# Stage one of a fused four-layer kernel written in another order: values four batches behind, block splits in two parts, later tables, two more banks

## The chip, the core and the metric

The kernel runs on one core of one Trainium2 chip. The time is that of the device in microseconds (us); lower is better. The profile comes from one profiled execution of the program, and its times count from the start of the span.

## The reference

Input x has 8 batches of 128 tokens with 512 features. Four layers are added to it one after the other. All arithmetic is fp32; the kernel builds each fp32 product from rounded parts (below).

```python
x = x + _L0_cond_ref(x, L0_cond_weight, itok_B_3_7)     # einsum('bsi,boi->bso', x, weight[ids]): one 512x512 weight for each batch
x = x + _L1_cond_ref(x, mask, pos, itok_B_0_7, wq, wk, wv, wo, aq, bq, ak, bk, av, bv, ao, bo)
x = x + _L2_cond_ref(x, A, B, itok_B_3_7)               # a rank-16 pair for each batch
x = x + _L3_cond_ref(x, itok_B_0_23, W, b, lora_As, lora_Bs)
...
def _L1_cond_ref(...):                                   # attention, 32 query heads, 8 key/value heads, D = 128
    q = lora_linear(x, wq, aq, bq, ids)                  # x @ w + (x @ a[ids]) @ b[ids]
    k = lora_linear(x, wk, ak, bk, ids)
    v = lora_linear(x, wv, av, bv, ids)
    q, k = apply_rope(q), apply_rope(k)                  # needs cos and sin of the positions
    ...                                                  # masked softmax(q k^T) v, then lora_linear(o, wo, ao, bo, ids)
```

## The kernel before, in words

The program has four parts, each an instruction block that all engines leave together. Stage one (up to about 118 us) computes layer L0 for the 8 batches and turns the result into what attention reads, and it also computes half of v. Stage two projects the rest of v and all of k. Then comes a loop over the 8 key/value heads, and last the layers L2 and L3. The change touches only stage one.

An fp32 product is built from three matmuls in the type fp32r: high x high, high x low, low x high. The high part of a tile is a copy by ScalarE (ACT), the low part is the difference, by VectorE (DVE) or GpSimd (POOL). In stage one the work on batch `b` is:

- SyncE (SP) loads x of the batch (`x_row(b)`, the tensor `res`), the batch's own 1 MB weight (`w0_raw`, shown as `w_raw`) and its adapter (`a_raw`). The weight has two buffers, so the load of batch b waits until the splits of batch b-2 are done.
- TensorE (PE) turns x (`turn_x`, into `ps_x`), ACT and DVE split it (`split_x`). ACT splits the four quarters of the weight; DVE takes the low part of quarters 0 and 2, POOL of 1 and 3 (`split_w`, both write `wt_lo`).
- `product`: 12 matmuls into `ps_y`. `add` (DVE, writes `res`): x1 = x + product. `turn_x1` (PE) and `split_x1` (ACT, DVE) give x1 turned, in two parts.
- `adapters` (PE, 12 matmuls of 48 columns, into `ps_a`), `pack_ax` (DVE, `axn`), `turn_ax` (PE), `copy_axt` (ACT, `axt_q`, `axt_k`, `axt_v`).
- `values`: PE runs `v_tile`, 13 matmuls of 512 columns into `ps_v`, ACT takes `v_hi`, DVE takes `v_lo`, SP stores both (`store_v`).

`v_tile` of batch 0 to 7 multiplies with block 0 of wv. A block is 1 MB of weight (`raw_w`, split into `blk_hi` and `blk_lo`) and 1 MB of adapter packs (`raw_b`, eight loads, split into `blk_b`: ACT one copy and DVE one `low_copies` on L169 for each of four packs). `block_part(0)` is this split of block 0, `block_part(1)` that of block 1, which stage two reads first. In block 1 the same tensors appear as `wt_x` and `wt_lo`. The rotation tables are computed by `angles` (DVE, four parts), two Sin activations (ACT), and the mask by `mask_table` (DVE).

The order is written out by hand: on each engine a loop over `b` calls these functions, and an engine does its instructions in that order. So whatever stands ahead of an instruction on its engine holds it up, however early its own inputs are. In the kernel before, PE does in iteration b: `turn_x(b + 1)`, `product(b)`, `turn_ax(b - 2)`, `adapters(b - 1)`, `values(b - 2)`, `turn_x1(b)`.

## Time and profile before

| | |
|---|---|
| time, median of 3 runs | 799.65 us (797.23 to 800.19) |
| the profiled execution: time | 800.8 us |
| the profiled execution: span | 799.1 us |
| PE busy in the span | 736.8 us (92%) |
| mean granted PE clock | 0.97 of full speed |
| stage one ends, first matmul of stage two | 118.20 us |

The page gives busy time by engine. For a change in one stage its rows are read by stage: what each engine did between two times, what it waited for, and in what order of time. A wait of PE in the middle of a stage costs its length only if PE is what the stage waits for later as well.

### The profile page before, as it was taken

The page shows a single profiled execution, that of the slowest core. Times are in us where ns is not written, and L with a number is a line of the kernel's source. Part 1 is how long each engine was busy: PE and PEld are TensorE (multiplying, and loading weights), DVE is VectorE, ACT ScalarE, POOL GpSimd, SP SyncE. Part 2 cuts the span into 40 slices and gives each one's busy share as a digit, 9 for nine tenths or more (in the row PEclk, how much of TensorE's full clock was granted, in tenths as well). Part 3 has the DMA queues.
Part 4 walks back from the last instruction along what each step waited for, and adds up shares of the span by engine and source line. Part 5 has one row for each costly group of instructions (what it writes and reads, how often), then busy time and mean ns, then how long its engine had stood idle before and what let it go on. Part 6 is the DMA issues. An engine that isn't in the chain of part 4 may idle for free. (4 is left out here: it accounts for less than half of the span.)

```text
span 799.1 us, 14134 instructions
## 1 busy us (share of the span) xinstructions
PE 736.8 (92%) x4392; PEld 646.8 (81%) x4392; DVE 549.0 (69%) x1468; ACT 328.0 (41%) x980; POOL 288.4 (36%) x242
## 2 busy tenths in 40 slices
PE   3597979998789999999999999999999999986898
PEld 2476858787679989998999998989999999876686
DVE  4667544688587676767677668767676767754973
ACT  3525343211154363445345445345445434443540
POOL 3322213245273254245236235325434522410510
PEclk9879979999899999999999999999999999999899
DMA  8557157865214024122212403402402112500402
GB/s 287 196 182 230 53 157 204 244 226 191 71 53 126 1 74 134 47 73 101 76 45 80 125 0 125 125 0 81 143 25 72 52 46 57 123 13 28 109 27 79
DMA packets 61435, 81.56 MB, mean 102 GB/s; under 512 B 21158, under 2 KB 38694, under 8 KB 57814
## 3 DMA queue, kind: packets, MB, share of 16 engines
q1 hardware_dynamic: 60482, 79.80, 32.2%
q0 software_dynamic: 768, 1.25, 0.6%
q8 instruction: 18, 0.29, 0.2%
q14 instruction: 19, 0.16, 0.1%
q10 hardware_dynamic: 148, 0.07, 0.0%
HBM read 66.13 MB, written 15.48 MB: 102 GB/s over the span
## 5 line engine op out<-in xcount | busy, mean ns | idle before, releaser
L1000 POOL TENSOR_TENSOR prob<-prob,rinv 128x512 f32<-128x512 f32 x64 | 66.7, 1042 | 199.7 <-DVE rinv L1090 199.7
L949 ACT ACTIVATE prob<-sm,nmax 128x128 f32<-128x128 f32 x256 | 99.8, 391 | 70.1 <-DVE nmax L1071 70.1
L1175 PE MATMUL ps_out<-wt_x,v_hi 128*128 128x272 f32 x512 | 112.8, 301 | 5.1 <-DVE v_lo L1043 2.7
L993 POOL TENSOR_TENSOR qt<-qc,qs 128x512 f32<-128x512 f32 x60 | 77.6, 1293 | 107.2 <-DVE qs L1026 107.2
L1179 PE MATMUL ps_out<-wt_x,v_lo 128*128 128x272 f32 x512 | 106.4, 289 | 0.0
L1177 PE MATMUL ps_out<-wt_lo,v_hi 128*128 128x240 f32 (+1 forms) x512 | 103.2, 283 | 0.0
L77 PE MATMUL ps_q<-x1t_hi,blk_hi 128*128 128x512 f32 x240 | 100.6, 419 | 0.0
L935 ACT ACTIVATE v_hi<-ps_o 128x512 fp32r<-128x512 f32 x64 | 38.1, 596 | 149.8 <-PE ps_o L1155 149.8
L79 PE MATMUL ps_q<-x1t_hi,blk_lo 128*128 128x512 f32 x240 | 95.7, 399 | 0.0
L78 PE MATMUL ps_q<-x1t_lo,blk_hi 128*128 128x512 f32 x240 | 95.6, 398 | 0.0
L1175 PEld LDWEIGHTS ps_out<-wt_x,v_hi 128*128 128x128 f32 x512 | 79.9, 190 | 9.3 <-DVE v_lo L1043 4.3
L1026 DVE TENSOR_TENSOR qs<-ps_q,sin_t 64x512 f32<-64x512 f32 x120 | 82.7, 689 | 3.7
L1177 PEld LDWEIGHTS ps_out<-wt_lo,v_hi 128*128 128x128 f32 x512 | 81.1, 190 | 0.0
L1179 PEld LDWEIGHTS ps_out<-wt_x,v_lo 128*128 128x128 f32 x512 | 79.6, 190 | 0.0
L1071 DVE CUSTOM_DVE_ANT_0 sm<-ps_s,maskbias 128x128 f32<-128x128 f32 x256 | 59.0, 286 | 29.6 <-issue 29.0
L1137 PEld LDWEIGHTS ps_s<-kt,qt 128*128 128x128 f32 x512 | 67.2, 193 | 11.4 <-issue 6.5
L1137 PE MATMUL ps_s<-kt,qt 128*128 128x128 f32 x512 | 68.4, 277 | 5.2 <-PEq L655 5.2
L929 ACT ACTIVATE v_hi<-ps_t 128x512 fp32r<-128x512 f32 x64 | 38.2, 597 | 43.6 <-PE ps_t L1145 43.6
L1050 DVE TENSOR_TENSOR res<-ps_out,res 128x272 f32<-128x272 f32 x128 | 49.9, 431 | 8.9 <-PE ps_out L1179 8.9
L79 PEld LDWEIGHTS ps_q<-x1t_hi,blk_lo 128*128 128x128 f32 x240 | 45.5, 190 | 10.9
L1039 DVE TENSOR_TENSOR v_lo<-ps_t,v_hi 128x512 fp32r<-128x512 f32 x64 | 44.1, 689 | 14.0 <-ACT v_hi L929 13.5
L77 PEld LDWEIGHTS ps_q<-x1t_hi,blk_hi 128*128 128x128 f32 x240 | 45.9, 191 | 8.3
(217 smaller groups left out, 1571.1 us busy)
## 6 DMA issues: line engine op xcount, KB each, us to landing
wo_raw<-in_L_cond_wo_l SPq DMA_DIRECT2D x8, 1024.0 KB, 4.7
raw_w<-in_L_cond_wq_l SPq DMA_DIRECT2D x8, 1024.0 KB, 5.3
raw_b<-in_L_cond_bq SPq DMA_DIRECT2D x64, 128.0 KB, 2.9
w_raw<-in_L_cond_weight_t SPq DMA_DIRECT2D x7, 1024.0 KB, 6.1
v_hi_d<-v_hi SPq DMA_DIRECT2D x16, 256.0 KB, 2.7
v_lo_d<-v_lo SPq DMA_DIRECT2D x16, 256.0 KB, 3.3
k_rot<-kr SPq DMA_DIRECT2D x16, 256.0 KB, 2.9
kt<-k_rot SPq DMA_DIRECT2D x16, 256.0 KB, 2.7
```

The source lines that it names most:

```text
L77: pe.matmul(bank[:, :], w_hi[:, k, cols], x1t_hi[:, k, tok], start=(k == 0), stop=False)
L78: pe.matmul(bank[:, :], w_hi[:, k, cols], x1t_lo[:, k, tok], start=False, stop=False)
L79: pe.matmul(bank[:, :], w_lo[:, k, cols], x1t_hi[:, k, tok], start=False, stop=False)
L949: e = act.activation(prob[i][:, h, :], sm[:, h, :], ACT.Exp, bias=nmax[i][:, h:h + 1], scale=-1.0, accum_out=rsum[i][:, h:h + 1])
L993: pool.tensor_tensor(qt[:, half, h, :], qc[:, :], qs[:, :], ALU.add).then_inc(q_done, 1)
L1000: pool.tensor_tensor(prob[i][:, :, :], prob[i][:, :, :], rinv[i][:, :].unsqueeze(2).broadcast_to([P, G, T]), ALU.mult).then_inc(prob_done, 1)
L1026: dve.tensor_tensor(qs[to:to + 64, :], ps_q[i][at:at + 64, :], sin_t[to:to + 64, tok], ALU.mult).then_inc(q_mult, 1)
L1071: m = dve.tensor_tensor_reduce(out=sm[:, h, :], in0=ps_s[i][:, h, :], in1=maskbias[:, b, :], scale=-1.0, scalar=3.0e38, op0=ALU.add, op1=A ...
L1137: mm = pe.matmul(ps_s[b % 2][:, h, :], qt[:, half, h, at:at + T], kt[:, b * T:(b + 1) * T], start=True, stop=True)
L1175: pe.matmul(ps_out[i][:, :], ot_hi[:, q], wo_x[:, h, wide], start=(h == 0), stop=False)
L1177: pe.matmul(bank, ot_hi[:, q], wo_lo[:, h, cols], start=False, stop=False)
L1179: mm = pe.matmul(ps_out[i][:, :], ot_lo[:, q], wo_x[:, h, wide], start=False, stop=(h == G - 1))
```

## The change

No computation is added or left out. Stage one is written in another order:

- `values` runs four batches behind (`LAG = 4`) where it ran two behind. The last four batches' tiles go to the two banks of `ps_y` in place of `ps_v`, since the products are over by then.
- `block_part` is cut into `block_w_part` (the weight) and `block_b_part` (the packs). For block 0 they stand in iterations 2 and 3 (both stood in 1), for block 1 in iterations 8 and 9 (both in 8), and behind the values of the iteration on ACT and DVE.
- SP loads x of batch 1 ahead of the weight of batch 1; the adapters and x of 2 and 3 next; block 0's weight behind the weight of batch 2; block 0's packs behind that of batch 3; block 1 behind that of batch 6.
- `angles` has one part in each of iterations 4 to 7 (two in each of 2 and 3); the two Sin activations stand in iteration 9 (4); `mask_table` in 10 (5).

```diff
+        LAG = 4
...
+            v_bank = [ps_v] * LAG + [ps_y[n % 2] for n in range(LAG, B)]
...
+                        if b == 0:
+                            sp.dma_start(x_row(1), x[1]).then_inc(x_in[1], 16)
                         if b == 1:
-                            for n in (1, 2, 3):
-                                sp.dma_start(x_row(n), x[n]).then_inc(x_in[n], 16)
-                            load_block_w(sp, 0)
                             sp.wait_ge(ids_in, 32)
                             picks.extend(...)
                             load_a(0)
                             load_a(1)
-                            load_block_b(sp, 0, picks)
+                            for n in (2, 3):
+                                sp.dma_start(x_row(n), x[n]).then_inc(x_in[n], 16)
                         if b == 2:
+                            load_block_w(sp, 0)
                             for n in range(4, B):
                                 sp.dma_start(x_row(n), x[n]).then_inc(x_in[n], 16)
                         if b >= 2:
                             load_a(b)
-                        if b == 5:
+                        if b == 3:
+                            load_block_b(sp, 0, picks)
+                        if b == 6:
                             sp.wait_ge(raw_lo_done, KC // 2 + PAIRS)
                             sp.wait_ge(raw_lo_pool, KC // 2)
                             load_block_w(sp, 1)
                             load_block_b(sp, 1, picks)
-                        if b >= 4:
-                            sp.wait_ge(v_lo_done, b - 3)
-                            store_v(sp, b - 4)
-                    for n in range(B - 4, B):
+                        if b >= LAG + 2:
+                            sp.wait_ge(v_lo_done, b - LAG - 1)
+                            store_v(sp, b - LAG - 2)
+                    for n in range(B - LAG - 2, B):
...
-                        if b == 1:                                  # POOL: block_lo(1, 0), block_lo(3, 0)
+                        if b == 3:
...
-                        else:                                       # PE, values(b)
+                        elif b < LAG:
                             pe.wait_ge(v_lo_done, b)
+                        elif b >= LAG + 2:
+                            pe.wait_ge(v_lo_done, b - 1)
                         pe.wait_ge(axt_done, 3 * b + 3)
-                        v_tile(pe, ps_v, 0, b, v_ready)
+                        v_tile(pe, v_bank[b], 0, b, v_ready)
...
-                        if b >= 2:
-                            values(b - 2)
+                        if b >= LAG:
+                            values(b - LAG)
...
                         if b == B:                                  # ACT
-                            block_part(1)
-                        if b >= 2:
-                            values(b - 2)
+                            block_w_part(1)
+                        if b == B + 1:
+                            block_b_part(1)
...
-                        if b == 1:
-                            block_part(0)
-                        if b == 4:
+                        if b == 2:
+                            block_w_part(0)
+                        if b == 3:
+                            block_b_part(0)
+                        if b == B + 1:
                             act.wait_ge(tab, 8)                     # then the two Sin activations
...
-                        if b in (2, 3):                             # DVE
-                            angles(2 * (b - 2))
-                            angles(2 * (b - 2) + 1)
-                        if b == 5:
+                        if 4 <= b < 8:
+                            angles(b - 4)
+                        if b == B + 2:
                             mask_table()
```

The queue of SP at the start of stage one, from the weight of batch 1 on, before (`res` is x, `raw_w` block 0's weight; L273 are loads of the adapter ids into registers, of which two of eight stand here):

```order
L267 DMA w_raw<-in_L_cond_weight_t 128x2048
L270 DMA res<-in_x 128x512 x3
L150 DMA raw_w<-in_L_cond_wv_l 128x2048
L273 TENSOR_LOAD id_rows
L273 ISA x2
L273 TENSOR_LOAD id_rows
```

The same queue in the changed kernel, from the second adapter load (`a_raw`) on:

```order
L256 DMA a_raw<-in_L_cond_a_qkv 128x192
L280 DMA res<-in_x 128x512 x2
L262 TENSOR_LOAD id_rows
L262 ISA x2
L271 DMA w_raw<-in_L_cond_weight_t 128x2048
L150 DMA raw_w<-in_L_cond_wv_l 128x2048
L284 DMA res<-in_x 128x512 x4
```

Block 0's weight now stands behind the weight of batch 2; before, it and all eight pack loads stood ahead of it.

DVE before, from the end of iteration 1 (`x1t_lo` of batch 1) to the sum x1 of batch 2 (`res`) and the tables:

```order
L509 TENSOR_TENSOR x1t_lo<-ps_x1turned,x1t_hi 128x4x128
L514 TENSOR_TENSOR a_lo<-a_raw,a_hi 128x192
L565 TENSOR_TENSOR blk_lo<-raw_w,blk_hi 128x512 x2
L169 SCALAR_TENSOR_TENSOR blk_b<-blk_b,rope_cols,raw_b 128x512 x4
L493 TENSOR_TENSOR xt_lo<-ps_x,xt_hi 128x512
L499 TENSOR_TENSOR wt_lo<-w_raw,wt_hi 128x512 x2
L504 TENSOR_TENSOR res<-ps_y,res 128x512
```

DVE in the changed kernel, from the same instruction on:

```order
L524 TENSOR_TENSOR x1t_lo<-ps_x1turned,x1t_hi 128x4x128
L529 TENSOR_TENSOR a_lo<-a_raw,a_hi 128x192
L508 TENSOR_TENSOR xt_lo<-ps_x,xt_hi 128x512
L514 TENSOR_TENSOR wt_lo<-w_raw,wt_hi 128x512 x2
L519 TENSOR_TENSOR res<-ps_y,res 128x512
L539 CAST axn<-ps_a 128x3x16 x2
L542 TENSOR_TENSOR axn<-ps_a,axn 128x3x16 x2
L524 TENSOR_TENSOR x1t_lo<-ps_x1turned,x1t_hi 128x4x128
L529 TENSOR_TENSOR a_lo<-a_raw,a_hi 128x192
L580 TENSOR_TENSOR blk_lo<-raw_w,blk_hi 128x512 x2
```

The sum of batch 2 no longer stands behind the six block operations.

ACT before, at the end of stage one, from the split of block 1 (`wt_x`) on (`v_hi` are the last two batches' values):

```order
L458 ACTIVATE wt_x<-raw_w 128x512 x4
L461 ACTIVATE blk_b<-raw_b 128x512 x4
L451 ACTIVATE v_hi<-ps_v 128x512
L440 ACTIVATE axt_q<-ps_at 128x128
L440 ACTIVATE axt_k<-ps_at 128x128
L440 ACTIVATE axt_v<-ps_at 128x128
L451 ACTIVATE v_hi<-ps_v 128x512
```

ACT in the changed kernel, from the values of batch 4 on:

```order
L460 ACTIVATE v_hi<-ps_y 128x512
L467 ACTIVATE wt_x<-raw_w 128x512 x4
L449 ACTIVATE axt_q<-ps_at 128x128
L449 ACTIVATE axt_k<-ps_at 128x128
L449 ACTIVATE axt_v<-ps_at 128x128
L460 ACTIVATE v_hi<-ps_y 128x512
L472 ACTIVATE blk_b<-raw_b 128x512 x4
L500 ACT_TABLE_LOAD
L500 ACTIVATE sin_t<-sin_t 128x1024
L501 ACTIVATE cos_t<-cos_t,rope_cols 128x1024
L460 ACTIVATE v_hi<-ps_y 128x512 x2
```

The last two `v_hi` now stand behind the pack split and the Sin activations.

## Rows read from the trace of the kernel before

**Rows 1.** The page, part 1: busy us, share of the span, instructions.
```profile
PE 736.8 (92%) x4392; PEld 646.8 (81%) x4392; DVE 549.0 (69%) x1468; ACT 328.0 (41%) x980; POOL 288.4 (36%) x242
```

**Rows 2.** Windows: stage one; the loop over heads (start:end, length, busy by engine, clock, DMA).
```profile
0.00:118.20 118.20, 83.95 (x384) 68.54 (x385) 71.93 (x112) 50.51 (x110) 33.84 (x28) 0.88 0.56 183
213.00:736.00 523.00, 511.40 (x3336) 464.26 (x3336) 369.20 (x1187) 237.43 (x793) 202.53 (x168) 0.99 0.23 69
```

**Rows 3.** Waits of PE in stage one: us in total, times, longest.
```profile
PE ps_x L333 <- DMA res<-in_x: 11.8, 2, 7.9
PE ps_x1turned L357 <- DVE res L504: 9.3, 4, 3.4
PE ps_y L347 <- POOL wt_lo L315: 4.6, 1, 4.6
```

**Rows 4.** Timeline, 12 to 21 us: start, length, engine, what, idle before.
```profile
13.70 2.53 POOL L315 TENSOR_TENSOR wt_lo<-w_raw,wt_x 128x512 fp32r<-128x512 f32 x2
15.32 4.54 DVE L499 TENSOR_TENSOR wt_lo<-w_raw,wt_hi 128x512 fp32r<-128x512 f32 x2
19.78 0.68 DVE L504 TENSOR_TENSOR res<-ps_y,res 128x512 f32<-128x512 f32 x1
20.18 0.35 SPq L267 DMA_DIRECT2D w_raw<-in_L_cond_weight_t  x1
```

**Rows 5.** DMA issued alone (us to landing), and the window 20 to 30 us.
```profile
w_raw<-in_L_cond_weight_t SPq DMA_DIRECT2D x1, 1024.0 KB, 4.8
20.00:30.00 10.00, 6.04 (x37) 5.45 (x38) 4.82 (x12) 3.53 (x7) 0.00 (x0) 0.94 1.03 368
```

**Rows 6.** Timeline, batches 1 and 2, 26 to 44 us.
```profile
26.00 2.19 ACT L424 ACTIVATE wt_x<-w_raw 128x512 fp32r<-128x512 f32 x4 [3.45 <-DMA w_raw<-in_L_cond_weight_t]
33.99 6.80 DVE L169 SCALAR_TENSOR_TENSOR blk_b<-blk_b,rope_cols,raw_b 128x512 fp32r<-128x512 f32 x4
36.92 0.79 PE L347 MATMUL ps_y<-wt_x,xt_hi 128*128 128x512 f32 x1 [4.63 <-POOL wt_lo L315]
43.00 0.68 DVE L504 TENSOR_TENSOR res<-ps_y,res 128x512 f32<-128x512 f32 x1
```

**Rows 7.** Windows: nine product matmuls, `adapters`, one iteration, a DVE iteration without tables.
```profile
36.92:40.93 4.01, 4.01 (x10) 3.14 (x11) 4.01 (x4) 0.84 (x2) 4.01 (x3) 0.50 0.24 61
41.46:43.98 2.52, 2.52 (x13) 2.52 (x14) 2.22 (x3) 0.61 (x3) 0.47 (x1) 0.50 0.67 270
83.79:92.13 8.34, 8.34 (x50) 7.10 (x48) 7.44 (x11) 4.52 (x11) 3.95 (x2) 1.00 0.21 63
68.44:76.45 8.01, 6.61 (x41) 5.45 (x39) 4.59 (x11) 5.34 (x8) 0.00 (x0) 1.00 0.42 129
```

**Rows 8.** Timeline: the longest part of the tables on DVE, and PE's last iterations.
```profile
55.04 3.45 DVE L545 SCALAR_TENSOR_TENSOR sin_t<-cos_t,sin_t 128x1024 f32<-128x1024 f32 x2
100.04 0.60 PE L357 MATMUL ps_x1turned<-ident,res 128*128 128x128 f32 x4
107.99 0.40 PE L184 MATMUL ps_v<-blk_b,axt_v 128*128 128x512 f32 x1
```

**Rows 9.** Timeline: the Sin activations, and the end of stage one.
```profile
72.55 1.28 ACT L485 ACT_TABLE_LOAD   x1
74.81 1.13 ACT L486 ACTIVATE cos_t<-cos_t,rope_cols 128x1024 f32<-128x1024 f32 x1
103.77 2.21 ACT L461 ACTIVATE blk_b<-raw_b 128x512 fp32r<-128x512 f32 x4
108.43 0.60 ACT L451 ACTIVATE v_hi<-ps_v 128x512 fp32r<-128x512 f32 x1 [2.45 <-PE ps_v L184]
109.06 0.69 DVE L560 TENSOR_TENSOR v_lo<-ps_v,v_hi 128x512 fp32r<-128x512 f32 x1
111.40 5.07 SPq L156 DMA_DIRECT2D raw_b<-in_L_cond_bk  x8
118.20 0.76 PE L181 MATMUL ps_p<-wt_x,x1t_hi 128*128 128x512 f32 x1 [2.95 <-PEq L246]
```

More of the change, by code:

```diff
@@ L310, in _ @@
                     pool.dma_start(mask_u8[:, :], mask.rearrange("b t -> (b t)").partition_broadcast(P)).then_inc(tables_in, 16)
-                    for b in range(B + 2):
+                    for b in range(B + 1):
                         if b < B:
@@ L387, in values @@
                             pe.wait_ge(raw_lo_pool, KC // 2)
-                        else:
+                        elif b < LAG:
                             pe.wait_ge(v_lo_done, b)
+                        elif b >= LAG + 2:
+                            pe.wait_ge(v_lo_done, b - 1)
                         pe.wait_ge(axt_done, 3 * b + 3)
-                        v_tile(pe, ps_v, 0, b, v_ready)
+                        v_tile(pe, v_bank[b], 0, b, v_ready)
                     turn_x(0)
-                    for b in range(B + 2):
+                    for b in range(B + LAG):
                         if b + 1 < B:
@@ L398, in _ @@
                             product(b)
-                        if b >= 2:
+                        if 2 <= b < B + 2:
                             turn_ax(b - 2)
@@ L450, in values, with block_w_part @@
                             act.wait_ge(v_out[b % 2], 32 * (b // 2))
-                        act.activation(v_hi[b % 2][:, :], ps_v[:, :], ACT.Copy).then_inc(v_hi_done, 1)
-                    def block_part(n):
+                        act.activation(v_hi[b % 2][:, :], v_bank[b][:, :], ACT.Copy).then_inc(v_hi_done, 1)
+                    def block_w_part(n):
                         act.wait_ge(raw_w_in, 16 * (n + 1))
@@ L458, in block_part, with block_b_part @@
                             act.activation(blk_hi[n][:, k, :], raw_w[:, k, :], ACT.Copy).then_inc(raw_hi_done, 1)
+                    def block_b_part(n):
                         act.wait_ge(raw_b_in, 16 * B * (n + 1))
@@ L464, in _ @@
                     split_w(0)
-                    for b in range(B + 2):
+                    for b in range(B + LAG):
                         if b + 1 < B:
@@ L470, in _ @@
                             split_a(0)
-                        if b >= 2:
+                        if 2 <= b < B + 2:
                             copy_axt(b - 2)
+                        if b >= LAG:
+                            values(b - LAG)
                         if b == B:
-                            block_part(1)
-                        if b >= 2:
-                            values(b - 2)
+                            block_w_part(1)
+                        if b == B + 1:
+                            block_b_part(1)
                         if b < B:
@@ L559, in values, with block_w_part @@
                         dve.wait_ge(v_hi_done, b + 1)
-                        dve.tensor_tensor(v_lo[b % 2][:, :], ps_v[:, :], v_hi[b % 2][:, :].bitcast(F32), ALU.subtract).then_inc(v_lo_done, 1)
-                    def block_part(n):
+                        dve.tensor_tensor(v_lo[b % 2][:, :], v_bank[b][:, :], v_hi[b % 2][:, :].bitcast(F32), ALU.subtract).then_inc(v_lo_done, 1)
+                    def block_w_part(n):
                         for k in (0, 2):
@@ L565, in block_part, with block_b_part @@
                             dve.tensor_tensor(blk_lo[n][:, k, :], raw_w[:, k, :], blk_hi[n][:, k, :].bitcast(F32), ALU.subtract).then_inc(raw_lo_done, 1)
+                    def block_b_part(n):
                         for p in range(PAIRS):
@@ L574, in _ @@
                     split_w(0)
-                    for b in range(B + 2):
+                    for b in range(B + LAG):
                         if b + 1 < B:
@@ L582, in _ @@
                             split_a(0)
-                        if b == B:
-                            block_part(1)
                         if 1 <= b <= B:
                             pack_ax(b - 1)
-                        if b >= 2:
-                            values(b - 2)
+                        if b >= LAG:
+                            values(b - LAG)
+                        if b == B:
+                            block_w_part(1)
+                        if b == B + 1:
+                            block_b_part(1)
                         if b < B:
@@ L592, in _ @@
                             split_a(b + 1)
-                        if b == 1:
-                            block_part(0)
-                        if b in (2, 3):
-                            angles(2 * (b - 2))
-                            angles(2 * (b - 2) + 1)
-                        if b == 5:
+                        if b == 2:
+                            block_w_part(0)
+                        if b == 3:
+                            block_b_part(0)
+                        if 4 <= b < 8:
+                            angles(b - 4)
+                        if b == B + 2:
                             mask_table()
```

## The prediction

> **What bounds the kernel now.** I read the page first: PE is busy 92% of the span [rows 1]. Then the stages: in the loop over heads PE is busy 511 of 523 us, but in stage one only 84 of 118 [rows 2]. So stage one holds 34 us in which PE has nothing to do, and it is the only stage that the change touches. What PE waits for there [rows 3]: 11.8 us for x, of which 7.9 us for one batch; 9.3 us for the sum x1 of a batch by DVE; 4.6 us for POOL's low half of a weight.
>
> The timeline shows that the long waits come from order, not from load. The weight of batch 2 is issued at 20.18, after SP has issued the packs of block 0 [rows 4]; ACT waits for it until 26.00. PE waits for POOL until 36.92. The sum of batch 2 comes at 43.00, because DVE did the packs first, 6.80 us from 33.99 on [rows 6]. And after its waits PE runs at half its clock: from 36.92 to 43.98 it is busy and the granted clock is 0.50, 1.2 GHz, against 1.00 in the iteration from 83.79 to 92.13 [rows 7]. So a wait costs twice.
>
> **The first batches.** POOL begins its splits at 13.70, when the weight of batch 1 has landed [rows 4]. x of batch 1 now goes ahead of that weight, 0.25 MB at the 368 GB/s of a full queue [rows 5], so POOL begins 0.7 us later. PE no longer sits before the product of batch 0 until x of batch 1 comes, but that product's second quarter needs POOL, so it ends about 0.7 us later too. The 7.9 us wait mostly changes its name: worth 0. The sum of batch 0 was done at 19.78 + 0.68 = 20.46 [rows 4], behind DVE's splits; I take 20.9.
>
> The weight of batch 2 needs POOL's two operations for batch 0, over at 13.70 + 2.53 = 16.2 [rows 4], now 17.0. SP is free then, so it is issued at about 17.2, and a 1 MB load alone lands in 4.8 us [rows 5]: 22.0, not 26.0. ACT's four splits take 2.2 us [rows 6], to 24.2. DVE and POOL take their halves beside each other. DVE's two operations took 4.54 us beside POOL's [rows 4], and alone they would take 2 x 0.69 [rows 9]; I take them as done at 26.2, and the sum of batch 1 at 26.9.
>
> The Trainium skill (SBUF — State Buffer, "Who interferes with whom") says that a VectorE instruction with two inputs in SBUF and a GpSimd instruction that reads SBUF do not run beside each other: the later one waits for the whole of the other. The 4.54 us [rows 4] agrees with it.
>
> Batch 2: the six DVE operations and POOL's two for block 0 no longer stand ahead. PE turns x1 and x (2 x 0.6 at most [rows 8]) and begins the product at 28; before, it came to the second part of it only at 36.92. I take it at half clock, since PE has idled 2 to 3 us. Nine matmuls of it took 4.01 us at that clock [rows 7], so twelve take 5.3: 33.3. The weight of batch 3 is now the last of about 3.1 MB behind that of batch 2 (block 0's weight, x of 4 to 7, an adapter, itself): at 368 GB/s 8.5 us, landing at 30.5. ACT splits it to 33, DVE ends at 34 and adds batch 2 by 34.7, where it was 43.68 [rows 6].
>
> **To the first values.** At half clock `adapters` takes 2.5 us [rows 7]. With the turns, adapters(1) ends at 36.3, product(3) at 42.6, adapters(2) at 45.6. DVE fits block 0's weight half (1.4 us) and the sum of batch 3 in by 43.7, so PE is the limit and stays busy. The packs' four DVE operations follow at 48: at least 4 x 0.69 = 2.8 us, at most the 6.80 of before, where POOL's four operations lay beside them; now POOL has two, later, so I take 3.4, to 51.4. Product(4) and adapters(3) end between 51, if the full clock comes back after 46, and 54. Then values(0), 13 matmuls, 3.0 us at the full clock (half of 0.45 each). I take its end as 55.0; 51.4 if PE has the full clock from 30 on, 59 if it has half until then.
>
> **The full iterations.** One with everything in it took 8.34 us, turn to turn [rows 7]. From values(0) to values(2) are two: 16.7. The next has no x to turn: 92.13 to 100.04, 7.9. The one to values(4) has no product: 100.04 to 107.99 + 0.40, 8.4 us, part of it at half clock [rows 8]. So values(4) ends at 88.0, and values(5), with `turn_ax` 3.3 us, at 91.3.
>
> The tables' cover: DVE without tables is busy 4.59 us in an iteration [rows 7]. The longest of the four parts adds 3.45 [rows 8]: 8.04 of 8.34. So they are hidden, at 0. Without the cover each part costs what exceeds it, at most 3.45. SP holds the weight of batch 7 behind block 1's nine issues (some 5.6 us) and a store of batch 0's values; it is issued at about 59 and needed at 65, so 0.
>
> **The end.** ACT has now, after values(5): `v_hi` 0.6, block 1's packs 2.1, table load and two Sin activations 3.4 (72.55 to 74.81 + 1.13), `v_hi` of batch 6 0.6; then DVE 0.7 [rows 9]. That is 7.3 us, where PE alone would need 3.0 and the two copies 1.3. So the Sin activations, in iteration 4 before, are on the path here for 3 us. `v_lo` of batch 6 is done at 98.6, where it was 109.75 [rows 9]. From there nothing changes: SP stores it, loads block 2 (eight pack issues, 5.07 us), stores batch 7, and stage two starts 118.20 - 109.75 = 8.45 us later [rows 9]. `mask_table`, now ahead of the last `v_lo`, lies beside SP's issues: 0; it was no wait of PE in [rows 3] either. Stage two starts at 107.05 instead of 118.20: 11.15 less. [...]
>
> **The sum.** 8.98 us are gained by the sum of batch 2 (43.68 to 34.7); the rest comes from work that fills PE's waits, less two tiles of values that are done later than before, less 3 us for Sin. In all -10.85. The profiled execution took 800.8 us, 1.15 above the median of 799.65; both have the same stages, so I take it from the median: 788.8.
>
> **Rivals.**
> 1. *As summed,* 0.55: 785 to 793.
> 2. *The clock comes back early,* 0.15: values(0) ends at 51.4, and the iteration to values(4) loses its slow part (1.6 us): 5 less, 784. For it: fewer long waits. Against it: PE still idles 2 to 3 us ahead of batch 2, and the short matmuls of `adapters` lay in the slow stretch of [rows 7] too.
> 3. *DVE becomes the limit in iterations 4 to 7,* 0.17: only 0.3 us of slack is left there, and POOL's splits of each batch can hold one of DVE's. At 1 to 1.5 us in four iterations the time is 793 to 795. The page's rule above makes this case, as four of the tables' eight operations read two SBUF tiles. Against more: from 83.79 to 92.13 DVE was busy 7.44 beside POOL's 3.95, and PE never stopped [rows 7].
> 4. *No difference,* 0.07: the weights of batches 3 to 5 land late behind the blocks' loads, and values(0) ends at 63 to 66: 797 to 800.
> 5. *Slower,* 0.06: PE stays at 1.2 GHz for all of stage one, because each iteration contains a short wait. An iteration then takes 5.3 for the product, 2.5 for `adapters`, 5.8 for values, and some 1.9 for the turns, 15.5 instead of 8.34: 7 more each. The gain is gone at two such iterations; with three it is 809.
>
> The range from 782 to 796 leaves some 0.15 outside; the first case's own is 785 to 793. About 0.5% (4 us) is what a measurement can tell from no change. Faster by more 0.88, within 0.07, slower 0.05.
>
> **What would show it.** Stage two's first matmul at 105 to 109. The weight of batch 2 landing near 22, `res` of batch 2 done near 35, no wait of PE for POOL, full clock from about 50 on. In iterations 5 to 7 PE goes from values to `turn_x1` without a stop; if it stops there for DVE, case 3 holds. `v_hi` of batch 6 right behind the Sin activations, and 8.4 us from `v_lo` of batch 6 to stage two. I am wrong if the weights of batches 3 to 5 come late, or if PE is at half clock still at 60.

## The result and the profile after

The changed kernel takes 791.16 us, median of 4 runs (786.26 to 791.78), beside 799.45 (797.23 to 800.19) for the kernel before: a ratio of 0.9883 (0.9849 to 0.9918). 788.8 was predicted, in a range of 782 to 796. The profiled execution took 791.78 us, its span is 790.1.

The page of the changed kernel, and its windows: stage one; stage two; the loop over heads with what follows it.

```profile
PE 728.6 (92%) x4392; PEld 641.0 (81%) x4392; DVE 546.5 (69%) x1468; ACT 327.8 (41%) x980; POOL 287.7 (36%) x242
```

```profile
0.00:108.12 108.12, 74.51 (x384) 61.54 (x385) 69.60 (x112) 50.47 (x110) 33.03 (x28) 0.94 0.64 201
108.12:205.90 97.78, 89.22 (x384) 71.91 (x384) 64.61 (x94) 17.68 (x32) 38.94 (x36) 0.95 0.63 195
206.00:790.10 584.10, 564.88 (x3624) 507.50 (x3624) 412.34 (x1262) 259.57 (x839) 215.74 (x178) 0.99 0.23 70
```

Against [rows 1] and [rows 2]: stage one has the same 384 matmuls, but they are busy 74.5 us instead of 84.0, and the stage is 10.1 us shorter. Its granted clock is 0.94 instead of 0.88. The clock accounts for the 9.4 us of busy time: an estimate from windows of 2 us (busy time of PE times what its granted clock lacks to 1.00) gives 12.5 us lost to the lower clock before and 2.6 after. PE's idle time as a whole is nearly the same, 33.6 us instead of 34.25, but it lies elsewhere. Without the wait ahead of stage two it fell from 31.3 to 23.9 us, and that wait grew from 2.95 to 9.7. So the change took 7.4 us of waiting out of the middle of the stage and put 6.8 at its end, and what the shorter stage has gained is nearly all clock.

PE's waits in stage one of the changed kernel (us in total, times, longest):

```profile
PE ps_x1turned L364 <- DVE res L519: 10.5, 6, 5.0
PE ps_p L181 <- PEq L250: 9.7, 1, 9.7
PE ps_x L340 <- DMA res<-in_x: 9.2, 2, 5.3
PE ps_y L354 <- POOL wt_lo L322: 2.9, 1, 2.9
PE ps_a L375 <- DVE x1t_lo L524: 1.3, 1, 1.3
```

Against [rows 3], the waits for x and for POOL are 2.6 and 1.7 us shorter. The wait for a sum is no shorter (10.5 for 9.3). And there is one of 9.7 us at the end, ahead of stage two, where 2.95 stood [rows 9]. One wait of the kernel before is gone, that of `v_tile` for ACT's copy `axt_v` of the same batch, which values two batches behind need almost at once:

```profile
PE ps_v L181 <- ACT axt_v L440: 3.5, 2, 2.7
```

The timeline of the changed kernel, rows of several engines in order of time:

```profile
14.32 2.50 POOL L322 TENSOR_TENSOR wt_lo<-w_raw,wt_x 128x512 fp32r<-128x512 f32 x2
14.59 5.24 DVE L514 TENSOR_TENSOR wt_lo<-w_raw,wt_hi 128x512 fp32r<-128x512 f32 x1 [0.35 <-ACT wt_hi L433]
16.78 2.50 POOL L322 TENSOR_TENSOR wt_lo<-w_raw,wt_hi 128x512 fp32r<-128x512 f32 x2
24.45 2.19 ACT L433 ACTIVATE wt_x<-w_raw 128x512 fp32r<-128x512 f32 x4 [1.78 <-DMA w_raw<-in_L_cond_weight_t]
28.15 0.66 PE L364 MATMUL ps_x1turned<-ident,res 128*128 128x128 f32 x4 [2.41 <-DVE res L519]
29.00 0.48 PE L354 MATMUL ps_y<-wt_x,xt_hi 128*128 128x512 f32 x1
31.86 0.45 PE L387 MATMUL ps_at<-ident_r,axn 128*128 128x128 f32 x3
34.87 2.19 ACT L433 ACTIVATE wt_hi<-w_raw 128x512 fp32r<-128x512 f32 x4 [4.07 <-DMA w_raw<-in_L_cond_weight_t]
37.83 0.68 DVE L519 TENSOR_TENSOR res<-ps_y,res 128x512 f32<-128x512 f32 x1
38.57 1.11 PE L364 MATMUL ps_x1turned<-ident,res 128*128 128x128 f32 x4 [4.96 <-DVE res L519]
56.24 0.60 ACT L460 ACTIVATE v_hi<-ps_v 128x512 fp32r<-128x512 f32 x1 [1.91 <-PE ps_v L184]
74.20 0.66 PE L364 MATMUL ps_x1turned<-ident,res 128*128 128x128 f32 x4 [0.23 <-DVE res L519]
92.38 0.60 ACT L460 ACTIVATE v_hi<-ps_y 128x512 fp32r<-128x512 f32 x1 [0.19 <-PE ps_y L184]
96.37 1.06 ACT L500 ACTIVATE sin_t<-sin_t 128x1024 f32<-128x1024 f32 x1
98.98 0.69 DVE L575 TENSOR_TENSOR v_lo<-ps_y,v_hi 128x512 fp32r<-128x512 f32 x1 [2.63 <-ACT v_hi L460]
108.12 0.76 PE L181 MATMUL ps_p<-wt_x,x1t_hi 128*128 128x512 f32 x1 [9.72 <-PEq L250]
```

The sum of batch 2 is done at 38.51 (before 43.68 [rows 6]), because the weight of batch 3 is split only from 34.87 on and DVE takes its low parts ahead of that sum. The product of batch 2 takes 2.86 us (29.00 to 31.86). From `v_hi` of batch 5 (92.38) to `v_lo` of batch 6 (99.67) it is 7.29 us, and from there to stage two 8.45.

### The profile page after: what moved, and what is told of

The parts are those of the page before. It is cut to its first block and busy times, and to the rows that moved or that the text cites. A ratio compares the mean times of both kernels' runs of the same rounds, so it can differ in the third digit from the quotient of the medians.

```text
span 790.1 us, 14134 instructions
## 1 busy us (share of the span) xinstructions
PE 728.6 (92%) x4392; PEld 641.0 (81%) x4392; DVE 546.5 (69%) x1468; ACT 327.8 (41%) x980; POOL 287.7 (36%) x242
## 5 line engine op out<-in xcount | busy, mean ns | idle before, releaser
L79 PE MATMUL ps_q<-x1t_hi,blk_lo 128*128 128x512 f32 x240 | 95.5, 398 | 0.0
L1157 PEld LDWEIGHTS ps_s<-kt,qt 128*128 128x128 f32 x512 | 67.1, 193 | 11.4 <-issue 6.5
L78 PEld LDWEIGHTS ps_q<-x1t_lo,blk_hi 128*128 128x128 f32 x240 | 45.7, 191 | 8.4
```

The costliest lines, as they stand in the source:

```text
L78: pe.matmul(bank[:, :], w_hi[:, k, cols], x1t_lo[:, k, tok], start=False, stop=False)
L79: pe.matmul(bank[:, :], w_lo[:, k, cols], x1t_hi[:, k, tok], start=False, stop=False)
L1157: mm = pe.matmul(ps_s[b % 2][:, h, :], qt[:, half, h, at:at + T], kt[:, b * T:(b + 1) * T], start=True, stop=True)
```

## The experiments

All are single edits of the changed kernel unless something else is said. With each ratio stands its interval.

### The loads around the weight of batch 3

`e1_packs_later`: SP issues the adapter packs of block 0 behind the weight of batch 4.

```diff
-                        if b == 3:
+                        if b == 4:
                             load_block_b(sp, 0, picks)
```

> The changed kernel with one line of SP moved: the eight pack loads of block 0 are issued behind the weight of batch 4 and no longer behind that of batch 3. Theory A: the weight of batch 3 comes late (ACT starts its split at 34.87, not at the 30.5 that I had summed) because the packs issued right behind it share the DMA engines with it, and they move slowly (212 to 220 GB/s between 30 and 34 us where the queue had moved 370 to 420 before). Then ACT starts that split at 31 to 32, the sum of batch 2 is done near 35.5 and not 38.5, and stage two starts 2 to 3.5 us earlier than 108.12. Rival B: it is late because of what stands ahead of it, block 0's weight and x of batches 4 to 7. Then ACT still starts it at 34 to 35 and nothing moves.

Measured: 786.57 us (786.18 to 786.98), 0.9817 (0.9784 to 0.985). The windows of the changed kernel, 20 to 34 us:

```profile
20.00:30.00 10.00, 6.96 (x44) 6.19 (x45) 6.11 (x13) 4.18 (x9) 2.95 (x2) 1.00 1.02 395
30.00:34.00 4.00, 3.61 (x24) 3.14 (x22) 1.22 (x3) 0.80 (x2) 0.00 (x0) 1.00 1.07 210
```

and from the timeline of the experiment:

```profile
30.21 2.19 ACT L433 ACTIVATE wt_hi<-w_raw 128x512 fp32r<-128x512 f32 x4 [0.60 <-DMA w_raw<-in_L_cond_weight_t]
103.38 0.77 PE L181 MATMUL ps_p<-wt_x,x1t_hi 128*128 128x512 f32 x1 [9.72 <-PEq L250]
```

Until 30 us the queue moves 395 GB/s. From 30 to 34 the packs share it, each onto 64 of the 128 partitions, and it moves 210, although the DMA engines are just as busy (1.07); in the experiment it was 341 in that stretch. So the weight, issued *ahead* of the packs, took 11.9 us to land, and 8.4 without them behind it. The sum of batch 2 was done 4.65 us earlier and stage two began 4.74 earlier: nothing on the way took it back. Theory A holds, with more than it had expected (2 to 3.5 us). But 1.2 of the 4.65 us lie ahead of the packs: SP issued this weight at 21.76 in the experiment and at 22.93 in the changed kernel. The Trainium skill (SBUF — State Buffer, "Door 1: The DMA port swizzle") says that a transfer onto 64 partitions reaches half of the memory's DMA ports. The 210 GB/s, about half of 395, agree with it. That a load ahead of such transfers also suffers is shown by the 11.9 and 8.4 alone.

The weight did not always suffer as much. Seven profiles have the packs right behind it, and it landed after 11.9 us (changed kernel), 11.4 (`e10_block0_together`), 10.5 (`e3_packs_in_stage_two`), 10.1 (`e5_tables_first`), 9.9 (`e6_one_bank`), 9.0 (`e4_x_behind_weight`) and 8.4 (`e2_sin_early`). In the two with the packs behind the next weight it was 8.4 and 8.1 (`e1_packs_later`, `e8_three`). The times agree: the changed kernel's four runs were 791.78, 786.26, 791.51 and 790.82 us; with the packs later all lay within 0.8 us. What decides how much the weight suffers in one execution stays open. In the experiments below, the time at which stage two begins in a single profile carries up to 4 us of this, so what an edit does is read from the differences behind the sum of batch 2, and from the medians.

`e7_weight3_first` goes further: besides, x of 5 to 7 and block 0's weight half are issued behind the weight of batch 3.

```diff
-                        if b == 2:
-                            load_block_w(sp, 0)
-                            for n in range(4, B):
-                                sp.dma_start(x_row(n), x[n]).then_inc(x_in[n], 16)
                         if b >= 2:
                             load_a(b)
                         if b == 3:
+                            sp.dma_start(x_row(4), x[4]).then_inc(x_in[4], 16)
+                            load_block_w(sp, 0)
+                            for n in range(5, B):
+                                sp.dma_start(x_row(n), x[n]).then_inc(x_in[n], 16)
+                        if b == 4:
+                            load_block_b(sp, 0, picks)
```

> The changed kernel with block 0's packs behind the weight of batch 4 (as in e1), and x of batch 4, block 0's weight and x of 5 to 7 behind the weight of batch 3. Theory A: the weight of batch 3 then comes some 4 us sooner than in e1 (2 MB less ahead of it at about 400 GB/s, 5 us, less the wait of its issue for the splits of batch 1), the sum of batch 2 is no longer set by it but by the product of batch 2, near 32.3 where e1 had 33.86, and stage two starts 1 to 2 us earlier than e1's 103.38. Rival B: block 0's weight, or x of a later batch, comes late in its place, and it is the same or slower than e1.

787.51 us (782.13 to 789.62), 0.9859 (0.9823 to 0.9895). The sum of batch 2 was done 1.5 us earlier than in `e1_packs_later`, and stage two began 1.5 earlier, as Theory A says, but in the fastest of its five runs (782.13), and the median is no better. Whether this order gains on top stays open here; `e11_four` below says no.

`e4_x_behind_weight`: x of batch 1 back behind the weight of batch 1.

```diff
-                        if b == 0:
-                            sp.dma_start(x_row(1), x[1]).then_inc(x_in[1], 16)
                         if b == 1:
+                            sp.dma_start(x_row(1), x[1]).then_inc(x_in[1], 16)
```

> The changed kernel with x of batch 1 issued behind the weight of batch 1, as before the change. Prediction: the early x of batch 1 is worth 0, since the product of batch 0 waits for POOL's low half, which starts when the weight of batch 1 has landed, so stage two starts within 0.5 us of 108.12. Rival: PE starts late and loses its clock, 1 to 2 us more.

789.4 us (785.81 to 792.92), 0.9862 (0.9809 to 0.9916): no difference from the changed kernel, as costed. PE now waits 12.8 us for x and not at all for POOL, where the changed kernel has 9.2 and 2.9: the wait changed its name. Stage two began at 104.23 and not within 0.5 us of 108.12, but this profile is one with the weight of batch 3 in early (9.0 us). Its four runs were 786.92, 792.92, 785.81 and 791.88, which lie wide apart too.

`e9_loads_as_before`: SP's whole queue up to the weight of batch 3 in the old order (x of 1 to 3, block 0's weight half, its packs and two adapters all behind the weight of batch 1); everything else as changed.

> The changed kernel with SP's queue up to the weight of batch 3 as it was before the change: x of 1 to 3 behind the weight of batch 1, then block 0's weight and, behind the first two adapters, its packs, all ahead of the weight of batch 2. Everything else, on all engines, is that of the changed kernel. Theory A: the gain came from the order on DVE, POOL and PE, not from the loads. The weight of batch 2 lands at 26.0 again, so the sum of batch 1 ends at 29 where it was 28.1, but the weight of batch 3 is in by 30 to 31, as all loads were before, and the sum of batch 2 ends at 34 to 35 where the changed kernel had 38.5: stage two starts at 103.5 to 105, up to 4.5 us earlier than 108.12, and the kernel takes 786 to 788. Rival B (as the prediction counted it): the early weight of batch 2 carries 4 us of the gain, and stage two starts at 110 or later.

790.85 us (788.81 to 791.12), 0.9893 (0.9859 to 0.9927), and stage two at 108.72. Both expectations missed (103.5 to 105, and 110 or later). The sum of batch 1 came late (30.27), as the old order makes it. But that of batch 2 was done at 36.62, 1.9 us *earlier* than in the changed kernel: the packs then stand ahead of the weight of batch 2, and ACT split the weight of batch 3 from 32.89 on without waiting for it. Two windows of this experiment:

```profile
30.40:36.00 5.60, 5.60 (x27) 4.99 (x27) 4.04 (x9) 3.65 (x8) 2.29 (x3) 0.75 0.73 265
82.00:90.00 8.00, 6.71 (x31) 5.70 (x31) 3.07 (x7) 1.39 (x5) 0.00 (x0) 0.79 0.22 68
```

The clock falls in both. The first lies ahead of the sum of batch 2. Of the lead of 1.9 us some 0.5 was left at `v_lo` of batch 0 (57.70 instead of 58.19; from 44 to 50 us the clock was at 0.50), and behind the second window it was gone: `v_lo` of batch 4 was done at 90.92 instead of 90.34. The new order of loads as a whole is worth nothing that can be measured.

### Which part of the change brings the time

`e12_values_behind_alone`: the kernel before, with only the values four batches behind, the two banks, and what the later order of block 1 needs. Loads, block 0 in one piece and early tables as before.

> One part of the change alone: values four batches behind, with the two banks, and the order of block 1 at the end. SP's queue up to the weight of batch 3, block 0's whole split in iteration 1 on ACT, DVE and POOL, the angles in iterations 2 and 3 and the Sin activations in iteration 4 are all as before the change. Theory A: the distance of the values alone gives little; it only makes it possible to move block 0's split and the tables, which is where the gain lies. DVE again does block 0 ahead of batch 2 and the tables ahead of batches 4 and 5, and PE, with no tile of values to do in iterations 2 and 3, waits there instead. Stage two starts at 114 to 118, since the Sin activations no longer stand at its end, and the kernel takes 796 to 800. Rival B: what counts is that PE's early products no longer stand behind tiles of values: stage two at 111 or earlier, 794 or less.

799.46 us (794.75 to 802.68, 10 runs), 0.9991 (0.9967 to 1.0014): no change, as Theory A says. Its profile is the fastest of the ten, 794.75 us, with stage two at 113.74. Its waits of PE in stage one:

```profile
PE ps_x1turned L361 <- DVE res L515: 12.4, 5, 6.0
PE ps_x L337 <- DMA res<-in_x: 11.0, 2, 7.1
PE ps_p L181 <- PEq L250: 7.0, 1, 7.0
PE ps_y L351 <- POOL wt_lo L319: 4.8, 1, 4.8
```

DVE still does packs and tables ahead of the sums, and PE waits for the sums. The wait for `axt_v` is gone, and that alone brings nothing.

`e5_tables_first`: the tables in iterations 2 and 3, the Sin activations in iteration 4, as before the change.

```diff
-                        if 4 <= b < 8:
-                            angles(b - 4)
+                        if b in (2, 3):
+                            angles(2 * (b - 2))
+                            angles(2 * (b - 2) + 1)
...
-                        if b == B + 1:
+                        if b == 4:
                             act.wait_ge(tab, 8)
```

> The changed kernel with the tables back where they were: two parts of angles in each of iterations 2 and 3 on DVE and the Sin activations in iteration 4 on ACT (mask_table stays late). Theory A (as predicted): in iterations 4 to 7 the tables are hidden, in 2 and 3 they are not, since there DVE comes late from the weight of batch 3: 6.6 us ahead of the sum of batch 3 and 5 us ahead of that of batch 4. The sum of batch 4 ends 8 to 11 us later than the changed kernel's 57.0, against 2.7 us given back at the end by the Sin activations; stage two starts 5 to 8 us later, 113 to 116, and the kernel takes 795 to 799. Rival B: DVE has room in 2 and 3 as well, and only the Sin activations count: 2 to 3 us faster than the changed kernel.

795.38 us (792.86 to 803.69, 10 runs), 0.9958 (0.9927 to 0.9989); stage two at 115.54, within Theory A's 113 to 116. The edit also takes the Sin activations off the end of the stage, which by itself brings 2.7 us (`e2_sin_early`), so the place of the tables is worth more than the difference shows.

`e10_block0_together`: both halves of block 0 are split in iteration 2 on ACT and DVE.

```diff
                         if b == 2:
                             block_w_part(0)
-                        if b == 3:
                             block_b_part(0)
```

> The changed kernel with both halves of block 0's split in iteration 2 on ACT and DVE (weight in 2 and packs in 3 in the changed kernel); the loads stay. Theory A: cutting it in two is worth little: the packs' 2.7 us on DVE go ahead of the sum of batch 3 instead of that of batch 4, and ACT and DVE wait a little for the packs to land; the sum of batch 4 ends at 57 to 59, where it was 57.0, and stage two starts 0 to 2 us later. Rival B: DVE's delay is paid in iteration 3 and not given back in 4, since PE takes its clock down after the wait: 3 us or more.

795.25 us (789.99 to 798.81, 10 runs), 0.9952 (0.9927 to 0.9976); stage two at 111.41. PE's wait for the sums, first in `e5_tables_first`:

```profile
PE ps_x1turned L364 <- DVE res L519: 15.5, 5, 7.7
```

then in `e10_block0_together`, with the packs on DVE, which stand ahead of the sum of batch 3 and take 4.77 us (2.74 in the changed kernel):

```profile
PE ps_x1turned L364 <- DVE res L518: 9.2, 4, 4.4
```

```profile
42.69 4.77 DVE L169 SCALAR_TENSOR_TENSOR blk_b<-blk_b,rope_cols,raw_b 128x512 fp32r<-128x512 f32 x4
```

With the tables first, the sum of batch 3 is done at 51.40, where the changed kernel has it at 47.59, and PE waits 5 us more for sums in all. With block 0 together it is done at 50.34. Here PE's waits for sums are no longer in all (9.2 for 10.5): the cost is the clock behind the one of 4.4 us. The stretch from 48 to 54 us, first in the experiment, then in the changed kernel:

```profile
48.00:54.00 6.00, 3.61 (x13) 3.22 (x14) 4.71 (x12) 2.39 (x6) 0.59 (x1) 0.50 0.49 184
```

```profile
48.00:54.00 6.00, 6.00 (x39) 5.32 (x38) 5.20 (x10) 5.66 (x13) 1.25 (x2) 1.00 0.67 203
```

`v_lo` of batch 0 is then done at 62.00 instead of 58.19, and stage two begins 3.3 us later: Theory A (0 to 2) missed, Rival B (3 or more) came. Each undoing costs some 0.7% of the time before (0.9958 and 0.9952 beside 0.9883), 4 us by the medians and 5.5 to 6 by the ratios. By the medians the two together are the whole gain of 8.3 us; by the ratios they are 11.5 of 9.4, so the two can't be told apart from a sum better than that. `e12_values_behind_alone`, which undoes both and the loads, lost all of it. Whether the tables could be put later with values only two batches behind was not tested; the packs could not, since `v_tile` of batch 0 reads them in iteration 2 there.

`e6_one_bank`: all values go through the one bank `ps_v`.

```diff
-            v_bank = [ps_v] * LAG + [ps_y[n % 2] for n in range(LAG, B)]
+            v_bank = [ps_v] * B
...
-                        elif b < LAG:
+                        else:
                             pe.wait_ge(v_lo_done, b)
-                        elif b >= LAG + 2:
-                            pe.wait_ge(v_lo_done, b - 1)
```

> The changed kernel with all values in the one bank ps_v, as before: values(b) on PE waits for v_lo of batch b-1. Theory A: the two banks for the last four batches are worth nothing here, because ACT reaches v_hi of batch 6 only behind the Sin activations; PE does values(5) 1.2 us later and values(6) 2 us later, but still about when ACT is ready: stage two starts 1.2 us later at most. Rival B: each of the last three tiles waits for two copies, 1.2 us each, and all three count: 3 to 4 us later.

788.52 us (786.22 to 793.89), 0.9868 (0.9821 to 0.9915). `v_lo` of batch 5 comes 1.3 us later behind that of batch 4 (4.70 instead of 3.37), but the step to batch 6 stays at 5.97: ACT's Sin activations, not the bank, stand there. Stage two began at 106.97, 8.4 us behind `v_lo` of batch 6, as in the changed kernel. No difference that can be measured.

### The end of stage one

`e2_sin_early`: the Sin activations one iteration earlier, between the copy for batch 6 and the values of batch 4.

```diff
+                        if b == B:
+                            act.wait_ge(tab, 8)
+                            act.activation(sin_t[:, :], ang[:, :], ACT.Sin).then_inc(sines, 1)
...
-                        if b == B + 1:
-                            act.wait_ge(tab, 8)
-                            act.activation(sin_t[:, :], ang[:, :], ACT.Sin).then_inc(sines, 1)
```

> The changed kernel with the two Sin activations moved from iteration 9 to iteration 8, ahead of the values of batch 4 on ACT, where ACT sat idle for 5.05 us. Theory A (as predicted): at the end they lie on the path; without them v_hi of batch 6 starts at PE's end of that tile, near 95.4 and not 98.38, and stage two starts 2.5 to 3 us earlier than 108.12. Rival B: another wait stands right behind it (the store of batch 4's values, or PE's tile): less than 1 us.

784.5 us (781.58 to 787.1), 0.9779 (0.974 to 0.9818). The `v_lo` of batches 5 and 6, and stage two, in this experiment:

```profile
88.83 0.69 DVE L575 TENSOR_TENSOR v_lo<-ps_y,v_hi 128x512 fp32r<-128x512 f32 x1 [0.38 <-ACT v_hi L460]
92.08 0.69 DVE L575 TENSOR_TENSOR v_lo<-ps_y,v_hi 128x512 fp32r<-128x512 f32 x1
101.22 0.77 PE L181 MATMUL ps_p<-wt_x,x1t_hi 128*128 128x512 f32 x1 [7.01 <-PEq L250]
```

3.25 us between them instead of 5.96: 2.7 gained, as costed. From 92.77 it is again 8.45 us to stage two. The other 4 us by which stage two is earlier are the early weight of batch 3 in this execution (the sum of batch 2 is done at 34.37 instead of 38.51). The median is 6.7 us lower, more than the term; how the rest divides between the weight of batch 3 and others, one profile can't say. The profile is that of the slowest of the four runs, 787.1, in which stage two took 99.9 us.

`e3_packs_in_stage_two`: SP issues the packs of block 2 as its first work of stage two, so behind the store of batch 7 and not ahead of it.

```diff
                             load_block_w(sp, 2)
-                            load_block_b(sp, 2, picks)
...
                 def _(sp):
+                    load_block_b(sp, 2, picks)
                     for n in range(N0, BLOCKS * UNITS):
```

> The changed kernel with the eight pack loads of block 2 moved from SP's end of stage one to SP's beginning of stage two. Theory A: the 8.45 us from v_lo of batch 6 to the first matmul of stage two are SP's issues, 5.06 of them for these loads, while no other engine needs the time. Then stage two starts at 103.5 to 104, bounded by the last v_lo at 102.26 and its two stores, 4 to 4.6 us earlier, and the packs, used 15 us later, still come in time. The whole time falls by 4 to 5 us. Rival B: the packs then land late in stage two and ACT waits for them, or the stage's stores stand behind the issues, so that the time falls by under 1 us.

785.61 us (784.7 to 788.3), 0.9801 (0.9768 to 0.9835): Theory A, with a stage two at 103.55. SP's queue at the end of stage one in the changed kernel:

```profile
100.73 0.49 SPq L150 DMA_DIRECT2D raw_w<-in_L_cond_wk_l  x1
101.32 5.06 SPq L156 DMA_DIRECT2D raw_b<-in_L_cond_bk  x8
106.75 0.38 SPq L175 DMA_DIRECT2D v_hi_d<-v_hi  x1
107.19 0.49 SPq L175 DMA_DIRECT2D v_lo_d<-v_lo  x1
```

and stage two in the experiment:

```profile
103.55 0.77 PE L181 MATMUL ps_p<-wt_x,x1t_hi 128*128 128x512 f32 x1 [5.26 <-PEq L250]
```

`v_lo` of batch 6 was done at the same time (99.57), and stage two followed in 3.98 us instead of 8.45. The eight issues cost 5.06 us of SP's time, and 4.47 of them come off the path: time in which PE, which goes on to stage two only with SP, had nothing to do.

`e8_three`: `e1_packs_later`, `e2_sin_early` and `e3_packs_in_stage_two` in one kernel.

> The changed kernel with e1, e2 and e3 together: packs of block 0 behind the weight of batch 4, the Sin activations ahead of the values of batch 4, packs of block 2 issued in stage two. Theory A: the three terms lie one behind the other, and add: v_lo of batch 6 at 92 to 92.5, the last v_lo 3 us later, stage two starts at 96 to 97; with up to 3 us lost again to the clock at the start of stage two the kernel takes 778 to 781. Rival B: they cover each other, or the start of stage two at half clock and its loads take them back: 783 or more.

779.43 us (777.65 to 781.28, 6 runs), 0.9747 (0.9718 to 0.9775). Its stage one and the first matmul of stage two:

```profile
0.00:96.10 96.10, 75.31 (x384) 62.30 (x385) 69.54 (x112) 50.49 (x109) 33.09 (x28) 0.98 0.66 212
```

```profile
96.12 0.77 PE L181 MATMUL ps_p<-wt_x,x1t_hi 128*128 128x512 f32 x1 [2.82 <-PEq L250]
```

In the profiles the terms add, as Theory A says: 4.7, 2.7 and 4.5 us are 11.9; stage two is 12.0 earlier and the median 11.7 lower. The medians of the three alone do not (4.6, 6.7 and 5.6 us lower, 16.8 in all), so part of what each showed by itself was not its own term. This version beats both kernels.

`e11_four`: that with the order of `e7_weight3_first`.

> e8 with the load order of e7 as well (x of 4, block 0's weight and x of 5 to 7 behind the weight of batch 3). Theory A: e7 started stage two 1.5 us earlier than e1, which adds here: stage two starts at 94.5 to 95.5, and the kernel takes 777 to 779.5. Rival B: as in the times of e7 (787.5 against 786.6 for e1), the clock's stretches in stage two take it back: 779 to 781, no difference from e8.

780.35 us (776.31 to 783.55), 0.9762 (0.9726 to 0.9797): no difference from `e8_three`. Stage two began at 98.82, 2.7 us later than there and not at 94.5 to 95.5. Theory A missed: the sum of batch 2 was done at 35.55, with PE at a clock of 0.50 from 28 to 32 us, where `e8_three` had 1.00 and 33.88. The time is Rival B's, but not for its reason: stage two took 96.2 us here and 96.8 in `e8_three`.

## Why the prediction was right, and where its terms were off

The main mechanism held: packs and tables out of the way of DVE's sums, fewer waits in the middle of the stage, PE at the higher clock for more of it. That the forecast came so close is in part luck, since several terms were off and the errors cancel.

- **Stage two earlier by 11.15: measured 10.08.** The span is 9.0 us shorter, where the sum gave 10.85. The 1.85 us between them are 1.1 in stage one and 1.3 in stage two (1.6, of which the sum has 0.3), less 0.5 in the rest of the kernel. The range and the direction held.
- **The weight of batch 2.** Issued at 17.04 (17.2 predicted). But ACT starts its splits at 24.45, not at 22.0: it took 7.4 us where the prediction had the 4.8 of a lone load. It was not alone. x of batches 2 and 3 had landed (3.1 us from 12.1 and 12.6), but POOL's loads of positions and mask, issued at 13.15 and 13.68, landed 4.8 and 5.4 us later, so beside it, and the queues moved only 178 GB/s from 17 to 19 us. Behind it stood block 0's weight, issued at 17.43. Which of these cost the 2.6 us was not tested.
- **Batch 2 "at half clock".** Wrong in this profile: PE idled 2.41 us ahead of it and kept the clock at 1.00, and the product took 2.86 us, not 5.3. But it is what came in others that have the same order up to there: after 1.77 us of idle time in `e5_tables_first`, 1.01 in `e6_one_bank` and 2.03 in `e10_block0_together` the granted clock from 28 to 32 us was 0.66, 0.64 and 0.50. So this term goes one way or the other from one execution to the next.
- **The weight of batch 3 "landing at 30.5".** This is the term that was mis-sized most. 3.1 MB at 368 GB/s left out what stands behind the weight in the queue. ACT began at 34.87, and the sum of batch 2 was done at 38.51 instead of 34.7. `e1_packs_later` shows most of the cause: the load takes 8.4 us without the packs behind it and 11.9 with them. The prediction named late weights as a sign of being wrong; this one came, and was paid for by the next point.
- **The clock from there on.** The full clock was back at 44 us, where the prediction had it after 46 (its second rival had it from 30 on). So the values of batch 0 ended only 1.2 us late (56.24 for 55.0).
- **The full iterations.** They took 8.80, 8.33, 8.36 and 6.65 us, by `v_lo`; 16.7 for the first two, 7.9 and 8.4 were predicted. The last is 1.75 us short, since PE kept its clock there, which is the other half of the second rival. This cancels most of what is late elsewhere: 0.4 and 0.5 us in the iterations before it, and some 1.9 us at `v_lo` of batch 0, which stands behind the sum of batch 4 on DVE. What is left at stage two is 1.1 us (108.12 for 107.05).
- **"8.98 us are gained by the sum of batch 2".** The attribution fell. It was 5.2 us earlier, and `e9_loads_as_before`, with the old loads, had it earlier still and was as fast as the changed kernel. What brings the time is that packs and tables no longer stand ahead of sums on DVE (`e5_tables_first`, `e10_block0_together`); the lag of four batches, alone worth 0, is what leaves room to put the packs later.
- **No wait of PE for POOL: wrong.** 2.9 us are left, at 15.65 in the product of batch 0, where the prediction's own text has the product wait for POOL.
- **The tables' cover: right.** In iterations 4 to 7 PE waits for a sum 0.86, 0, 0.23 and 0 us, and the first of these lies ahead of the tables. The rival in which DVE becomes the limit did not come.
- **The end: right.** 7.29 for 7.3 and 8.45 for 8.45, with Sin's term confirmed by 2.7 us of the 3 that it was costed at.
- **Stage two.** The sum takes 10.85 where stage two comes 11.15 us earlier; no run shows the 0.3 us between them. In the two profiles stage two took 1.6 us longer. The windows for its start, a stretch near its end, and (before) the loop and what follows:

Windows of the kernel before:

```profile
118.20:123.10 4.90, 4.90 (x16) 3.93 (x17) 0.69 (x1) 0.92 (x2) 1.50 (x3) 0.71 0.82 210
197.00:201.00 4.00, 4.00 (x19) 3.28 (x20) 2.57 (x5) 0.00 (x0) 2.59 (x2) 1.00 0.19 75
214.47:799.10 584.63, 565.62 (x3624) 507.84 (x3624) 412.33 (x1262) 259.74 (x839) 215.96 (x178) 0.99 0.23 70
```

Windows of the changed kernel at the same places of the program:

```profile
108.10:113.00 4.90, 4.88 (x14) 3.89 (x15) 0.69 (x1) 0.63 (x1) 1.50 (x3) 0.60 0.76 192
187.00:191.00 4.00, 4.00 (x11) 3.13 (x12) 1.78 (x3) 0.00 (x0) 2.50 (x2) 0.57 0.18 71
```

Stage two took 96.27 us before and 97.9 after; the rest 584.6 and 584.1. PE starts it after 9.7 idle us instead of 2.95 and does 14 matmuls instead of 16 in the first 4.9 us. A second fall near its end, at 0.57 where it was 1.00, costs more than the first (11 matmuls instead of 19). Its cause was not tested. Nor is the idle time ahead of the stage shown to cost anything: stage two took from 95.5 to 98.3 us in the six profiles with 9.7 us ahead of it (the changed kernel and experiments e1, e4, e7, e9 and e10) and from 96.2 to 97.9 in the four with 2.8 to 3.6 (the kernel before and e6, e8 and e11). The 1.6 us lie within that spread.

## What to carry to other kernels

Before you credit a gain to the load or wait that vanished, undo each part by itself: here the new order of the loads, which looked decisive, was as a whole worth nothing that can be measured, and the gain came from DVE's order ahead of the sums that PE waits for. Price a load by everything in its queue while it is under way, what is issued behind it too, and price DMA issues on SP as work where another engine goes on only with SP. And where a kernel was just reordered, read the chain again at its new end: the three edits that this showed (Sin, two groups of pack issues) gained more than the change itself.

## What the runs showed of the hardware that was not expected

- A 1 MB load was slowed by transfers issued behind it in the same queue, each onto 64 partitions: 8.4 to 11.9 us to landing in seven profiles, 8.4 and 8.1 in the two in which those transfers were issued some 5 us later.
- One DVE operation of 0.69 us took 5.24 (14.59 to 19.83), as long as POOL's four lasted (14.32 to 19.28), and 5.23 to 5.25 in the nine other profiles with x of batch 1 early. The Trainium skill (SBUF — State Buffer, "Who interferes with whom") has the later of two such instructions wait for the whole of the other. Here it waited for all four and not for one. Elsewhere in the same trace two DVE operations beside two of POOL took 2.86 us.
- The length of a short wait did not say whether TensorE's clock would fall. Ahead of batch 2 it stayed at 1.00 after 2.41 us of idle time in the changed kernel and after 2.30 in `e3_packs_in_stage_two`, and was at 0.50 behind 1.01 us in `e6_one_bank`, 2.03 in `e10_block0_together` and 2.53 in `e11_four`. Nor did a longer one go with a deeper fall: the first 4.9 us of stage two had 0.60 after 9.7 us idle in the changed kernel, 0.71 after as much in `e4_x_behind_weight`, 0.71 after 2.95 in the kernel before and 0.50 after 3.56 in `e6_one_bank`.
